# Covariance of the second layer: GpSimd's low parts of six of eight tiles behind the last centred tile, and one load of x issued later

## The chip, the cores and the metric

The kernel is one program on one core of a Trainium2 chip. The metric is the device time of one execution in microseconds. The kernel before takes 867.92 us (median of three runs, 866.33 to 868.16).

## The reference

Two layers, all in float32. The first computes attention weights per pixel and applies them to shifted copies of x; the second is a bottleneck of three convolutions with batch norms and a residual. The change lies in the second, between the second convolution and the end:

```
residual = x
h = relu(bn(conv(x, w1, 1x1), g1, b1))
h = relu(bn(conv(h, w2, 3x3), g2, b2))     # 64 channels
h = bn(conv(h, w3, 1x1), g3, b3)           # 256 channels
return relu(h + residual)                  # (4, 256, 64, 64)
```

`bn` takes mean and variance over batch, height and width of its own input, so the third one needs the statistics of `conv(h, w3)` before the first output can be written.

## The kernel before, in words

The five engines run their own instruction lists, written out by hand, and meet at semaphores (`wait_ge(name, count)`, `then_inc`). There is no scheduler: the order in the code of an engine's block is its order on the chip.

After the second convolution its output lies in `y`, 128 partitions (two groups of 64 channels) by 8 tiles of 1024 pixels. The third batch norm does not run the third convolution first. Its mean and variance are got from the sum of h and from the covariance (Gram) matrix of h, 64 by 64 for each half, through the weights. For that each tile i goes through these steps:

- ScalarE, L1063: batch norm and ReLU of the tile in place, its sum beside it (`relu2`);
- VectorE, L1842: subtracts a constant from the tile (centring), then L1844: casts it to `h2_hi`, the high part of a two-part float32 split. Each counts `centered` up by one, so tile i is done at `centered` 2i + 2;
- GpSimd, L842: the low part, `h2_lo = y - h2_hi`, from two operands in SBUF (`h2_lo_done`);
- TensorE, L1381: transposes each half tile k = 2i, 2i + 1 into PSUM (`hT_ps`), ScalarE L848 (`hT_hi`) and VectorE L1431 (`hT_lo`) split the transposed half, and TensorE L1389 adds it to the Gram matrix (`gram`). On ScalarE the two copies of a tile stand behind the ReLU of the next one.

`hT` has two buffers, so the copies of half tile k wait for the Gram group k - 2.

Then VectorE forms scale and shift of the third batch norm in a chain of small instructions, each waiting for the one before: L1848, L1850 and L1851 on the mean, ahead of the last two `hT_lo`; L1858 to L1865 on the Gram matrix; L1867, L1868, L1869, L1794, a root on ScalarE (L1033), L1797 to L1800. L1850, L1851 and L1794 are tensor_scalars on one or two columns, L1868, L1869 and L1798 to L1800 tensor_tensors with both inputs in SBUF.

The last stage has 32 groups m, four for each of eight output pieces u. TensorE (`last`, L1090 to L1092) multiplies the third weights with `h2_hi` and `h2_lo` of two tiles (0 and 1 for the first two u, 2 and 3 for the next two, and so on); there are four places in PSUM, so group m waits for the addition m - 3. VectorE L1878 scales it and adds x, in the place to which x was loaded (`x1in`, or `y[:, 4:8]` for u = 6). ScalarE L1082 adds the shift, applies the ReLU and writes the result into the place of the piece before (for u = 0 into `y[:, 0:4]`). SyncE stores half a piece after every second group (L509).

The residual x was written by the first layer to memory and comes back in eight loads of 2 MB on SyncE (L712), each issued when its place is free: the seventh (u = 6) goes to `y[:, 4:8]`, so it has to wait for the transposes and the low parts, the eighth for L1867. The stores follow on the same queue.

Of the kernel before, what the change touches and what calls it, by code (L numbers as in the profile page):

```python
# [118 lines left out]
def build(nc, x, w1, b1, w2, b2, v1, g1, c1, v2, g2, c2, v3, g3, c3, out):  # L119
# [6 lines left out]
    with top:  # L126
        def sem(name):
            return top.enter_context(nc.semaphore(name))
# [113 lines left out]
        def x1_place(u):  # L242

            return y[:, 4:8, :] if u == 6 else x1in[:, (2, 3, 4, 5, 6, 1, None, 0)[u], :, :]

        def out_place(u):

            place = x1_place(u - 1) if u else y[:, 0:4, :]
            return place.rearrange("p i e -> p (i e)").rearrange("p (r c) -> p r c", c=W)
# [32 lines left out]
        relu2, h2_lo_done = sem("relu2"), sem("h2_lo_done")  # L282
        c2_done, c2_copied, c2_stat = sem("c2_done"), sem("c2_copied"), sem("c2_stat")
        vT_done, center_done, cov_zero, centered = sem("vT_done"), sem("center_done"), sem("cov_zero"), sem("centered")
        hT_ps, hT_hi_done, hT_lo_done, gram_done = sem("hT_ps"), sem("hT_hi_done"), sem("hT_lo_done"), sem("gram_done")
# [219 lines left out]
        def store_out(sp, u):  # L505
            n, cb = u // 2, u % 2
            for h in range(2):
                sp.wait_ge(f_out, 4 * u + 2 * h + 2)
                sp.dma_start(out[n, cb * P:(cb + 1) * P, 32 * h:32 * h + 32, :],  # L509
                             out_place(u)[:, 32 * h:32 * h + 32, :]).then_inc(out_stored, 16)  # L510
# [17 lines left out]
        def _(sp):  # L528
# [181 lines left out]
            def load_x1(u):  # L710
                n, cb = u // 2, u % 2
                sp.dma_start(x1_place(u), x1_dram[4 * n:4 * n + 4, cb].rearrange("s p e -> p s e")).then_inc(x1_back[u], 16)  # L712
# [5 lines left out]
                load_x1(u)  # L718
            sp.wait_ge(c2_done, 16)
            load_x1(5)  # L720
            sp.wait_ge(hT_ps, 16)
            sp.wait_ge(h2_lo_done, 8)
            load_x1(6)
            sp.wait_ge(sums_ps, 1)
            sp.wait_ge(bn_dve, BN3_READ)
            load_x1(7)
            for u in range(8):
                store_out(sp, u)
            sp.wait_ge(out_stored, 16 * 16)

        @block.gpsimd
        def _(pool):
# [105 lines left out]
            pool.wait_ge(vt_done, 2)  # L838
            pool.memset(cov[:, :], 0.0).then_inc(cov_zero, 1)
            for i in range(8):  # L840
                pool.wait_ge(centered, 2 * i + 2)
                pool.tensor_tensor(h2_lo[:, i, :], y[:, i, :], h2_hi[:, i, :].bitcast(F32), ALU.subtract  # L842
                                   ).then_inc(h2_lo_done, 1)

        @block.scalar
        def _(act):
# [225 lines left out]
            for u in range(8):  # L1072
                cb = u % 2
                if u == 0:
                    act.wait_ge(hT_ps, 16)
                    act.wait_ge(h2_lo_done, 8)
                else:
                    act.wait_ge(f_out, 4 * u)
                for k in range(4):
                    h, a = divmod(k, 2)  # L1080
                    act.wait_ge(f_added, 4 * u + k + 1)
                    act.activation(out_place(u)[:, 32 * h + a:32 * h + 32:2, :].rearrange("p r (c b) -> p b r c", b=2),  # L1082
                                   x1_place(u)[:, 2 * a:2 * a + 2, h * HALF:(h + 1) * HALF].rearrange("p b (r c) -> p b r c", c=SW),
                                   ACT.Relu, bias=shift[:, 2 + cb:3 + cb]).then_inc(f_out, 1)
# [344 lines left out]
        def _(dve):  # L1429
# [328 lines left out]
            def prepare(a):  # L1758
                dve.wait_ge(v_hi_done, 4 * a + 4)
                dve.wait_ge(vT_done, a + 1)  # L1760
                rows = slice(64 * a, 64 * a + 64)
                for k in range(3 * a, 3 * a + 3):
                    (lo, ty), (hi, _) = v2_blocks(v2_lo)[k], v2_blocks(v2_hi)[k]
                    minus(lo, v2_of(rows, ty), hi.bitcast(F32)).then_inc(v_lo_done, 1)
                minus(v3_lo[rows, a, :], psR[1][rows, C:2 * C], v3_hi[rows, a, :].bitcast(F32)).then_inc(v_lo_done, 1)
# [140 lines left out]
```

## Time and profile before

| | |
|---|---|
| median of the runs | 867.92 us |
| profiled execution, its own time | 868.58 us |
| its span | 866.8 us |
| PE busy | 811.2 us (94%) |
| DVE, ACT, POOL busy | 649.2, 376.1, 346.7 us |
| granted clock, mean | 0.98 |
| DMA moved | 162.18 MB, mean 187 GB/s |

The profile is of one execution. PE is TensorE's matmul, PEld its weight load, DVE VectorE, ACT ScalarE, POOL GpSimd, SP SyncE. Times run from the start of the span. The shares are averages over very different stages: the first layer fills about 700 us, the second convolution ends at 774 us, the tiles are centred from 780.6 to 807 us, and the last stage goes from 818.6 us to the end. Only the last 90 us hold anything that the change touches. In these the page's 40 slices show PE at 6, 8, 9, 9 and 6 tenths, and DMA at 9 and more in the last stage but at 0 to 5 while the tiles are centred.

### The profile page before, as it was taken

How to read it: one execution, taken by the hardware profiler on the slowest of the kernel's cores; microseconds unless marked ns; L12 is line 12 of the kernel's file. 1: busy time of each engine (PE TensorE's matmuls, PEld its weight loads, DVE VectorE, ACT ScalarE, POOL GpSimd, SP SyncE). 2: the span in 40 equal slices, each digit the busy share in tenths (PEclk: the TensorE clock that was granted, in tenths of full speed). 3: DMA queues.
4: the chain of work that ended last, by engine and by line, in shares of the span. 5: the costliest groups of instructions: out<-in, count | busy, mean ns of one | idle time of the engine just before them, and what ended most of it. 6: DMA issues, size and time to landing. Idle time of an engine off the chain costs nothing.

```text
span 866.8 us, 13972 instructions
## 1 busy us (share of the span) xinstructions
PE 811.2 (94%) x5084; PEld 770.1 (89%) x5084; DVE 649.2 (75%) x884; ACT 376.1 (43%) x647; POOL 346.7 (40%) x256
## 2 busy tenths in 40 slices
PE   4998988999999999999999999999968989996896
PEld 4997988999999999999999999999968867775685
DVE  4895888898699589868968977896576667129796
ACT  1332112334343434434344444534246697116396
POOL 3318586385267248527723852772200010006200
PEclk9999999999999999999999999999989989998999
DMA  9920515986894996779499688747299995020598
GB/s 265 372 104 0 98 28 132 218 215 171 185 244 123 230 180 193 202 162 243 120 242 174 183 208 168 206 114 211 65 257 264 267 335 236 0 84 14 187 425 358
DMA packets 249932, 162.18 MB, mean 187 GB/s; under 512 B 191833, under 2 KB 232778, under 8 KB 247178
## 3 DMA queue, kind: packets, MB, share of 16 engines
q1 hardware_dynamic: 241162, 144.52, 63.6%
q10 hardware_dynamic: 8704, 16.78, 6.1%
q8 instruction: 42, 0.69, 0.4%
q14 instruction: 24, 0.20, 0.1%
HBM read 99.48 MB, written 56.36 MB: 180 GB/s over the span
## 4 chain that ended last, share of the span: by engine, by line
PE 75%; DVE 8%; issue 5%; POOL 5%; ACT 3%; DMA 3%; SPq 1%; ACTq 0%; DVEq 0%; POOLq 0%
PE ps L1090 21%; PE ps L1092 21%; PE ps L1091 21%; PE ps L1160 4%; PE ps L1176 3%; PE ps L1208 3%; POOL xbuf L778 2%; PE ps L1115 1%; POOL ring L767 1%; DMA w1raw<-in_L_conv_w 1%; DMA raw<-bands 1%; DVE y L1842 1%; POOL whole L762 1%; DVE whole L1519 1%; DVE wsum L1471 1%
## 5 line engine op out<-in xcount | busy, mean ns | idle before, releaser
L767 POOL TENSOR_TENSOR ring<-whole,ring 128x576 fp32r<-128x576 f32 x112 | 188.5, 1687 | 272.9 <-ACT ring L848 272.9
L1090 PE MATMUL ps<-w_hi,ring 128*128 128x336 f32 x832 | 277.7, 334 | 9.4 <-DVE me L1596 7.2
L1092 PE MATMUL ps<-w_hi,ring 128*128 128x336 f32 x832 | 265.3, 319 | 0.0
L1091 PE MATMUL ps<-w_lo,ring 128*128 128x336 f32 x832 | 264.2, 318 | 0.0
L1090 PEld LDWEIGHTS ps<-w_hi,ring 128*128 128x128 f32 x832 | 159.9, 192 | 10.2 <-issue 7.7
L1091 PEld LDWEIGHTS ps<-w_lo,ring 128*128 128x128 f32 x832 | 159.6, 192 | 0.0
L1092 PEld LDWEIGHTS ps<-w_hi,ring 128*128 128x128 f32 x832 | 158.7, 191 | 0.0
L848 ACT ACTIVATE ring<-whole 128x576 fp32r<-128x576 f32 x112 | 87.1, 778 | 107.1 <-POOL whole L762 58.1
L848 ACT ACTIVATE band_hi<-ps 128x320 fp32r<-128x320 f32 (+1 forms) x128 | 53.0, 417 | 127.5 <-PE ps L1160 121.3
L1519 DVE SCALAR_TENSOR_TENSOR whole<-xbuf 128x576 f32<-128x576 f32 x80 | 88.3, 1105 | 14.6 <-POOL ring L767 7.5
L1090 PE MATMUL ps<-band_hi,xT_hi 128*128 128x224 f32 (+2 forms) x320 | 94.9, 297 | 3.2 <-DVE band_lo L1431 3.1
L1091 PE MATMUL ps<-band_lo,xT_hi 128*128 128x224 f32 (+2 forms) x320 | 92.6, 289 | 0.0
L1092 PE MATMUL ps<-band_hi,xT_lo 128*128 128x224 f32 (+2 forms) x320 | 92.6, 289 | 0.0
L778 POOL TENSOR_TENSOR xbuf<-xbuf 128x1152 f32<-128x1152 f32 x32 | 86.5, 2704 | 1.3
L1431 DVE TENSOR_TENSOR band_lo<-ps,band_hi 128x320 fp32r<-128x320 f32 (+1 forms) x128 | 57.4, 455 | 21.5 <-ACT band_hi L848 21.1
L848 ACT ACTIVATE xT_hi<-ps 128x512 fp32r<-128x512 f32 x64 | 37.9, 595 | 79.9 <-PE ps L1176 78.6
L1090 PEld LDWEIGHTS ps<-band_hi,xT_hi 128*128 128x128 f32 x320 | 60.9, 190 | 5.5 <-DVE band_lo L1431 3.7
L1596 DVE SCALAR_TENSOR_TENSOR logit<-ps,logit 128x480 f32<-128x480 f32 x80 | 52.2, 653 | 18.0 <-PE ps L1092 14.4
L1090 PE MATMUL ps<-h_hi,v_hi 128*128 128x512 f32 x160 | 64.8, 405 | 0.6 <-DVE x1in L1878 0.4
L1091 PE MATMUL ps<-h_lo,v_hi 128*128 128x512 f32 x160 | 64.5, 403 | 0.0
L1092 PE MATMUL ps<-h_hi,v_lo 128*128 128x512 f32 x160 | 64.0, 400 | 0.0
L1431 DVE TENSOR_TENSOR xT_lo<-ps,xT_hi 128x512 fp32r<-128x512 f32 x64 | 43.5, 683 | 26.2 <-ACT xT_hi L848 26.2
(165 smaller groups left out, 1370.2 us busy)
## 6 DMA issues: line engine op xcount, KB each, us to landing
xq<-in_x SPq DMA_DIRECT2D x116, 256.0 KB, 4.9
raw<-bands SPq DMA_DIRECT2D x32, 768.0 KB, 7.1
xbuf<-in_x SPq DMA_DIRECT2D x16, 1024.0 KB, 8.7
x_dram<-x ACTq DMA_DIRECT2D x32, 512.0 KB, 4.7
x1in<-x_dram SPq DMA_DIRECT2D x7, 2048.0 KB, 13.3
bands<-wide SPq DMA_DIRECT2D x64, 199.0 KB, 5.4
out<-x1in SPq DMA_DIRECT2D x12, 1024.0 KB, 5.9
w1raw<-in_L_conv_w SPq DMA_DIRECT2D x2, 3136.0 KB, 12.7
```

Of the source, the lines that this page charges most:

```text
L767: pool.tensor_tensor(split(k, 1), positions(whole[:, k % TBUFS, :], 0, 2), split(k, 0).bitcast(F32), ALU.subtract).then_inc(sig_lo_done, 1)
L778: pool.tensor_tensor(a, b, a, ALU.subtract).then_inc(c_done, 1)
L848: return act.activation(dst, src, ACT.Copy)
L1090: pe.matmul(dst, l_hi, r_hi_, start=first, stop=False, **kw)
L1091: pe.matmul(dst, l_hi, r_lo_, start=False, stop=False, **kw)
L1092: return pe.matmul(dst, l_lo, r_hi_, start=False, stop=last, **kw)
L1160: mm = pe.transpose(bank[:, i * P:(i + 1) * P], src, ident[:, :])
L1176: mm = pe.transpose(bank[:, t * C + kb * P:t * C + (kb + 1) * P], src[:, kb, 4 * t:4 * t + 4, g % 2::2], ident[:, :])
L1208: mm = pe.matmul(bank, v1pack[:, cb, :], r[:, cb, :], start=(cb == 0 and j == 0), stop=(cb == CB - 1 and j == 1))
L1431: return dve.tensor_tensor(dst, a, b, ALU.subtract)
L1519: dve.scalar_tensor_tensor(out=dst, in0=a, scalar=factor, in1=b, op0=ALU.mult, op1=ALU.add).then_inc(done, 1)
L1596: dve.scalar_tensor_tensor(out=dst, in0=m, scalar=factor, in1=src, op0=ALU.mult, op1=ALU.add).then_inc(comb_done, 1)
```

## The change

Three edits:

- GpSimd's low parts of tiles 0 and 1 stay where they were. Those of tiles 2 to 7 wait until all eight tiles are centred and cast (`centered` 16) in place of their own tile.
- ScalarE's first instruction of the last stage, which overwrites tiles 0 to 3 of `y`, waits for four low parts in place of eight.
- SyncE's load of x for u = 6, with its two waits, moves from ahead of the load for u = 7 to behind the two stores of the first piece.

```diff
@@ -718,13 +718,14 @@
                 load_x1(u)
             sp.wait_ge(c2_done, 16)
             load_x1(5)
-            sp.wait_ge(hT_ps, 16)
-            sp.wait_ge(h2_lo_done, 8)
-            load_x1(6)
             sp.wait_ge(sums_ps, 1)
             sp.wait_ge(bn_dve, BN3_READ)
             load_x1(7)
             for u in range(8):
+                if u == 1:
+                    sp.wait_ge(hT_ps, 16)
+                    sp.wait_ge(h2_lo_done, 8)
+                    load_x1(6)
                 store_out(sp, u)
             sp.wait_ge(out_stored, 16 * 16)
 
@@ -838,7 +839,7 @@
             pool.wait_ge(vt_done, 2)
             pool.memset(cov[:, :], 0.0).then_inc(cov_zero, 1)
             for i in range(8):
-                pool.wait_ge(centered, 2 * i + 2)
+                pool.wait_ge(centered, 2 * i + 2 if i < 2 else 16)
                 pool.tensor_tensor(h2_lo[:, i, :], y[:, i, :], h2_hi[:, i, :].bitcast(F32), ALU.subtract
                                    ).then_inc(h2_lo_done, 1)
 
@@ -1073,7 +1074,7 @@
                 cb = u % 2
                 if u == 0:
                     act.wait_ge(hT_ps, 16)
-                    act.wait_ge(h2_lo_done, 8)
+                    act.wait_ge(h2_lo_done, 4)
                 else:
                     act.wait_ge(f_out, 4 * u)
                 for k in range(4):
```

SyncE's list at the end of the program (`x_dram` is the copy of x in memory, `y` the place of the load for u = 6; the first two rows are the loads for u = 1 to 4 and u = 5):

```order
 L712 DMA x1in<-x_dram 128x4x1024 x4
 L712 DMA x1in<-x_dram 128x4x1024 [waits c2_done]
-L712 DMA y<-x_dram 128x4x1024 [waits h2_lo_done,hT_ps]
 L712 DMA x1in<-x_dram 128x4x1024 [waits bn_dve,sums_ps]
 L509 DMA out<-y 128x2048 [waits f_out] x2
+L712 DMA y<-x_dram 128x4x1024 [waits h2_lo_done,hT_ps]
 L509 DMA out<-x1in 128x2048 [waits f_out] x12
 L509 DMA out<-y 128x2048 [waits f_out] x2
```

The load into `y` was ahead of the last load into `x1in` and of all stores; now it stands behind the last load and the stores of the first piece, and 14 stores are behind it.

VectorE's list behind the cast of tile 7, as it is in the changed program (all its lines are one further down than before; `gm` and `mv` hold a few columns of statistics, `scale` and `shift` the result):

```order
L1849 TENSOR_REDUCE gm<-sums 128x1
L1851 TENSOR_SCALAR gm<-gm 128x1 [waits bn_dve]
L1852 TENSOR_SCALAR gm<-gm 128x2 [waits bn_dve]
...
L1868 COPY gm<-ps 128x6 [waits sums_ps,bn_dve]
L1869 TENSOR_TENSOR gm<-gm 128x2 [waits bn_dve]
L1870 TENSOR_TENSOR gm<-gm 128x2 [waits bn_dve]
L1795 TENSOR_SCALAR mv<-gm 128x2 [waits bn_dve]
L1798 RECIPROCAL mv<-mv 128x2 [waits bn_act,bn_dve]
L1799 TENSOR_TENSOR scale<-mv,bn 128x2 [waits bn_dve]
L1800 TENSOR_TENSOR mv<-gm,scale 128x2 [waits bn_dve]
L1801 TENSOR_TENSOR shift<-bn,mv 128x2 [waits bn_dve]
L1879 SCALAR_TENSOR_TENSOR x1in<-ps,scale,x1in 128x2x512 [waits f_done,x1_back0,bn_dve]
```

These rows stand in the same order in both programs, and so do GpSimd's eight subtractions; what moved is that six of the eight now start behind the cast of tile 7, and so beside these rows, where there was one.

## Rows read from the trace of the kernel before

**Rows 1.** chain of waits, 776 to 822 us, shares of the stretch by line

```profile
by line: DVE y L1842 18.6%; DVE hT L1431 12.7%; PE ps L1389 9.5%; PE ps L1381 8.2%; issue 7.8%; DVE h_hi L1844 7.8%; ACT y L1063 5.6%; PE ps L1090 4.1%; PE ps L1091 3.6%; PE ps L1092 3.0%; DVE x1in L1878 2.8%; DVE gm L1851 2.1%; ACT hT L848
```

**Rows 2.** VectorE's L1842: durations in ns, least/median/longest

```profile
L1842 DVE TENSOR_SCALAR y<-y,gm x8: 748/1752/1901, 780.6 to 805.3; 128x1024 f32<-128x1024 f32 x8
```

**Rows 3.** timeline of GpSimd, 750 us on: start us, us, what, [idle before]

```profile
793.05 2.39 POOL L842 TENSOR_TENSOR h_lo<-y,h_hi 128x1024 fp32r<-128x1024 f32 x1 [1.36 <-DVE h_hi L1844]
...
808.02 2.38 POOL L842 TENSOR_TENSOR h_lo<-y,h_hi 128x1024 fp32r<-128x1024 f32 x1 [1.36 <-DVE h_hi L1844]
```

**Rows 4.** timeline of VectorE, 773 to 820 us (same columns)

```profile
794.36 1.63 DVE L1842 TENSOR_SCALAR y<-y,gm 128x1024 f32<-128x1024 f32 x1 [0.19 <-ACT y L1063]
796.03 0.69 DVE L1844 CAST h_hi<-y 128x1024 fp32r<-128x1024 f32 x1
...
809.49 0.93 DVE L1851 TENSOR_SCALAR gm<-gm 128x2 f32<-128x2 f32 x1
...
816.95 0.16 DVE L1868 TENSOR_TENSOR gm<-gm 128x2 f32<-128x2 f32 x1
...
818.64 2.48 DVE L1878 SCALAR_TENSOR_TENSOR x1in<-ps,scale,x1in 128x1024 f32<-128x1024 f32 x2
```

**Rows 5.** windows: length, busy PE PEld DVE ACT POOL, clock, DMA share, GB/s

```profile
830.00:834.00 4.00, 4.00 (x19) 3.22 (x18) 4.00 (x4) 4.00 (x4) 0.00 (x0) 1.00 1.02 428
...
865.00:866.00 1.00, 0.00 (x0) 0.00 (x0) 0.00 (x0) 0.00 (x0) 0.00 (x0) 0.50 0.36 148
```

**Rows 6.** timeline of ScalarE, 773 to 820 us

```profile
792.51 0.60 ACT L848 ACTIVATE hT<-ps 128x512 fp32r<-128x512 f32 x1 [0.56 <-PE ps L1389]
793.01 1.24 ACT L1063 ACTIVATE y<-y,shift,scale 128x1024 f32<-128x1024 f32 x1
...
799.20 0.60 ACT L848 ACTIVATE hT<-ps 128x512 fp32r<-128x512 f32 x1 [0.32 <-PE ps L1389]
```

**Rows 7.** timeline of TensorE, 773 to 820 us

```profile
785.58 1.12 PE L1381 MATMUL ps<-ident,y 128*128 128x128 f32 x4 [2.33 <-DVE h_hi L1844]
...
796.78 0.66 PE L1381 MATMUL ps<-ident,y 128*128 128x128 f32 x4 [1.43 <-DVE h_hi L1844]
...
798.38 0.72 PE L1389 MATMUL ps<-hT 128*128 128x256 f32 x4
...
819.98 0.50 PE L1090 MATMUL ps<-h_hi,v_hi 128*128 128x512 f32 x1 [0.41 <-DVE x1in L1878]
```

**Rows 8.** timeline of VectorE, 133 to 138 us

```profile
134.07 1.54 DVE L1633 TENSOR_TENSOR me<-smx,inside 128x112 f32<-128x112 f32 x1
135.65 2.85 DVE L1639 TENSOR_TENSOR wide<-probs,me 128x784 f32<-128x784 f32 x1
```

**Rows 9.** VectorE's L1633: durations in ns, least/median/longest

```profile
L1633 DVE TENSOR_TENSOR me<-smx,inside x8: 274/274/1544, 134.1 to 638.9; 128x112 f32<-128x112 f32 x8
```

**Rows 10.** timeline of GpSimd, 133 to 138 us

```profile
133.36 4.31 POOL L778 TENSOR_TENSOR xbuf<-xbuf 128x1152 f32<-128x1152 f32 x2
```

**Rows 11.** windows, the fall and return of the clock

```profile
785.00:786.00 1.00, 0.42 (x2) 0.43 (x3) 1.00 (x2) 0.15 (x2) 0.40 (x1) 0.50 0.00 0
...
791.00:792.00 1.00, 1.00 (x8) 1.00 (x7) 0.80 (x1) 0.76 (x3) 0.70 (x1) 0.68 0.00 0
```

**Rows 12.** page, part 6: DMA issues, KB each, us to landing

```profile
x1in<-x_dram SPq DMA_DIRECT2D x7, 2048.0 KB, 13.3
...
out<-x1in SPq DMA_DIRECT2D x12, 1024.0 KB, 5.9
```

**Rows 13.** timeline of SyncE's DMA issues, 750 us to the end

```profile
810.47 0.36 SPq L712 DMA_DIRECT2D y<-x_dram  x1
816.99 0.36 SPq L712 DMA_DIRECT2D x1in<-x_dram  x1
822.41 2.74 SPq L509 DMA_DIRECT2D out<-y  x2
...
859.25 3.11 SPq L509 DMA_DIRECT2D out<-y  x2
```

## The prediction

> **What bounds the kernel now.** I read the stretch behind the second convolution (776 us to the end) in this order: the chain of waits, the timelines of VectorE, GpSimd, ScalarE and TensorE, the granted clock, and last the DMA queue of SyncE. In the chain from 776 to 822 us the largest single item is the centring of the tiles, VectorE L1842, with 18.6% [rows 1]. It needs 0.75 us when nothing is in its way, but its median is 1.75 and its longest 1.90 [rows 2]. The reader is to hold two rows side by side: GpSimd's subtraction of 793.05 ends at 795.44 [rows 3], the centring issued at 794.36 ends at 795.99 [rows 4], 0.55 us later. So the centring does not run slowly, it stands until GpSimd's instruction is over and then runs. This is the time the change goes after. Behind it comes the last stage, 32 groups of matmuls, each followed by a VectorE addition, a ReLU and half a store. TensorE is busy in all of it (4.00 of 4.00 us at 830 to 834), VectorE's additions follow it, and the DMA engines are full beside it: share 1.02 and 428 GB/s in the same row [rows 5].
>
> **The sum is made** against the profiled execution: span 866.8, time 868.58, which is 0.66 above the median of 867.92. I write P for the start of GpSimd's last subtraction, 808.02 before [rows 3]; that is just when the last tile is centred and cast.
>
> **What goes: the blocked centrings.** GpSimd still does tiles 0 and 1 at their old places, so up to the centring of tile 2 nothing changes. The centring of tile 3 can start at 791.20 as before. From there a loop over two tiles sets the pace. Centring to cast 0.78 (its 0.75 and a gap), cast to the transposes of that tile 0.75 (796.03 to 796.78), transposes to the second Gram group 1.60 (796.78 to 798.38), Gram to ScalarE's copy 0.82 (to 799.20), copy to ReLU 0.50 (792.51 to 793.01), ReLU to centring 1.35 (793.01 to 794.36) [rows 4, 6, 7]: 5.80 us per two tiles. Tile 4 stays at 794.36, since its ReLU is what it waits for; tile 5 comes at 791.20 + 5.80 = 797.00, tile 6 at 800.16, tile 7 at 802.80 (before: 805.3 [rows 2]). With 0.78 and 0.77 behind it (cast to GpSimd's start), P comes at 804.35: **a gain of 3.65 us.** ScalarE and TensorE, not VectorE, are late next, which is why six freed waits of up to 1.15 us don't all come back.
>
> **What is added: a queue of six on GpSimd.** From P on GpSimd has six subtractions in a row, 2.38 us each [rows 3], 14.3 us in all; before it had one. VectorE's small instructions of the third normalisation lie in that time. One is known: L1851, two elements wide, took 0.93 us and ended at 810.42, GpSimd's instruction at 810.40 [rows 3, 4]. It costs the same in both kernels. The others came when GpSimd was done: L1868, L1869 and L1794 from P + 8.93 on (816.95), and the first addition of the last stage at P + 10.62 (818.64) [rows 4]. Now they meet GpSimd's fourth, fifth and sixth.
> Does a two-input instruction on VectorE stand behind GpSimd too, and who goes first when both queue? The softmax of the first layer shows both. L1633 takes 1.54 us at 134.07, where its least is 0.27, and L1639 right behind it 2.85 [rows 8, 9]; beside them stand two subtractions of GpSimd, 133.36 to 137.67 [rows 10]. Each of the two small ones waited for one of GpSimd's: VectorE gets in between two of them, and then the next of GpSimd's goes ahead of VectorE's next. Applied here: L1868 waits to P + 9.5, L1869 to P + 11.9, L1794 to P + 14.3. From L1794 to the first addition is 1.3 us (L1868, L1869 and L1794 follow each other by 0.20, and the addition follows L1868 by 1.69), so that starts at P + 15.5 and not P + 10.62: **a loss of 4.9 us**. From below: if two elements slip through, nothing is lost; if only one wait is met, 0.6 (L1868 against the fourth) to 2.4 (a whole one). From above: 12 us, if L1851 too must let all six pass. I take 4.9, since the row nearest in kind shows alternation.
> The Trainium skill (SBUF — State Buffer, Who interferes with whom) has the rule for it: the port pair is a lock for a whole instruction, taken by a VectorE instruction in a two-port mode, or with two SBUF inputs against a GpSimd instruction that reads SBUF. The trace agrees for 112 and 784 elements; for two-element tensor_tensors no row before shows it. By that page alone L1798 to L1800 would be at risk as well, but GpSimd is empty by then.
> Together: the last stage starts 4.9 − 3.65 = **1.25 us later**.
>
> **What follows on TensorE.** It computes four groups ahead and then waits for the first addition. That wait was 0.41 us, restart at 819.98 [rows 7]. It becomes about 0.41 + 4.9 = 5.3 us. After the idle stretch of 2.33 us that ended at 785.58 [rows 7] the granted clock was 0.50 at 785 to 786, and it came back inside 791 to 792 (0.68) [rows 11], so about 6 us behind the restart, at the lower of the two levels, 1.2 GHz. Six microseconds at half rate are **3.0 us** of TensorE work, and the last stage follows TensorE. Both ends: 0 (the clock stays), 3.5 (it stays down 7 us). End by TensorE: 866.8 + 1.25 + 3.0 = 871.05.
>
> **What follows for the DMA.** The load of x for tile group 6, 2048 KB [rows 12], went out at 810.47, when the engines were idle [rows 13]. Now it stands in SyncE's order behind both stores of the first output, so at about 826, in the full stretch. It is needed over 20 us later, so nothing waits for it; but all stores behind it do. Bytes from the first store on: 16 stores of 1.049 MB (1024 KB [rows 12]) and 2.10 MB, 18.9 MB, at 428 GB/s [rows 5] 44.1 us. The first store went out at 822.41 [rows 13], now 823.7. In the kernel before the last store is issued at about 862.0 [rows 13] and its bytes end at about 865.4 (148 of some 400 GB/s in 865 to 866 [rows 5]): 3.4 us, of which 2.45 are its 1.049 MB at 428, so 1.0 to the first byte; the span ends 1.4 later. Now the bytes end at 823.7 + 1.0 + 44.1 = 868.8: end by the DMA 870.2. TensorE's 871.05 is the later; with some backlog in front of the last store I take 871.2. Here the two costs cover each other: without the clock's loss the DMA would still hold the end at 870.2. Stores 2.8 us apart (the two issued in 859.25 to 862.36 [rows 13]) ask for 375 GB/s, so a backlog of 2.1 MB shrinks by only 50 GB/s, 1.0 MB in 20 us.
> The Trainium skill (SBUF — State Buffer, Summary: rules for kernel authors) would take 358 GB/s for transfers between HBM and SBUF. By it the 18.9 MB need 52.7 us and the span ends at 878.8. The trace disagrees: it holds 428 [rows 5].
>
> ScalarE's lowered wait (4 in place of 8) is met at P + 4.8, ahead of its first ReLU of the last stage; it only avoids a wait. The low parts of tiles 2 to 7 are wanted by TensorE 5.6 us behind its restart and later, when all are done.
>
> **Forecast:** span 871.2, 4.4 over before; 873.0 for the profiled execution, 872.3 on the scale of the median: slower by 0.5%. Its own range is 870.5 to 874 (clock cost 0 to 3.5, GpSimd's pitch).
>
> **Rivals.**
> 1. *The small instructions are hardly held* (two elements slip through, or one wait in all). For: no row has a two-element instruction with two inputs beside a subtraction of GpSimd. Against: L1851 and [rows 8]. With a loss of 0.6 the stage starts 3.05 earlier and TensorE would end at 863.75, but load 7, the stores and load 6 are then one stream of 21.0 MB, 49.0 us, from 816.99 − 3.65 + 1.0 = 814.3 on: 863.3 + 1.4 and 1.0 for the slower first microseconds of a load, 865.7; with 2.4 it is about 867.9. Time 866.8 to 869.0: mostly no change. 0.20.
> 2. *The DMA has room after all and nothing is held:* 866.8 − 3.65 + 0.6, time 864.9. Against: 428 GB/s is what the full stretch gives. 0.04.
> 3. *GpSimd's queue goes first every time,* place L1851: VectorE is let in at P + 14.3, the Gram matrix of the last tiles comes 12 us late, less 3.65, and 3 for the clock: time 879.2 (11.9 − 3.65 + 3.0 over 867.92). It decides if GpSimd's next instruction is taken ahead of a VectorE one already waiting. Against: [rows 8, 10]. 0.05.
> 4. *The stores are held to 358 GB/s,* as by the rule above: span 878.8, time 879.9. Against: [rows 5]. 0.02.
> 5. *The same mechanism, dearer:* the clock falls twice, or the addition instructions are held too: 874 to 876.5. 0.07.
> The forecast itself has 0.62.
>
> **How the numbers follow.** A change under 0.2% (1.7 us) can't be told from none. Slower: 0.62 + 0.05 + 0.02 + 0.07, 0.76, less 0.04 for the forecast's lower edge: 0.72. Rival 1 gives 0.10 to "same" (with the 0.04: 0.14) and 0.10 to "faster" (with rival 2: 0.14). The range goes from 867.0, inside rival 1, to 875.0, inside rival 5, and leaves out rivals 2 to 4 and part of 1.
>
> **What would show it.** Centrings of tiles 4 to 7 at 0.75 us, and GpSimd's third instruction starting near 804.4: right on the gain. L1868, L1869 and L1794 (each one line further down) with durations of up to 2.4 us: right on the loss. TensorE's idle time ahead of the first group that waits for an addition near 5 us and a clock of 0.50 behind it. 2.1 MB of loads amid the stores, DMA share 1.0 to the end, last store landing later than 4.8 us. The forecast is wrong if the small instructions keep 0.17 us beside a busy GpSimd.

## The result, and the profile after

The changed kernel takes **873.96 us** (median of 5, 873.55 to 876.65) where the kernel before takes 867.92 beside it (866.33 to 869.06): a ratio of **1.0084, 95% interval 1.0067 to 1.0100**, slower. The forecast was 872.3, 4.4 over the kernel before; 6.0 over it were measured, so the sign is right and the size 1.7 us short. The profiled execution took 876.65 (span 874.8), the slowest of the five; 873.0 was forecast for it, with a range of 870.5 to 874, and it lies above that. Of the 8.0 us by which its span exceeds that of the kernel before, 1.5 lie ahead of the first centring, where nothing was changed, and 6.5 behind it. Its lines behind SyncE's edit stand one further down: L1843 is L1842 before.

VectorE's timeline of the changed kernel (start us, us, engine, line, operation, [idle before], with rows left out at the dots):

```profile
792.58 0.75 DVE L1843 TENSOR_SCALAR y<-y,gm 128x1024 f32<-128x1024 f32 x1 [0.53 <-ACT y L1064]
795.17 0.74 DVE L1843 TENSOR_SCALAR y<-y,gm 128x1024 f32<-128x1024 f32 x1
...
807.21 0.93 DVE L1852 TENSOR_SCALAR gm<-gm 128x2 f32<-128x2 f32 x1
...
814.67 0.46 DVE L1869 TENSOR_TENSOR gm<-gm 128x2 f32<-128x2 f32 x1
815.16 2.32 DVE L1870 TENSOR_TENSOR gm<-gm 128x2 f32<-128x2 f32 x1
817.51 2.27 DVE L1795 TENSOR_SCALAR mv<-gm 128x2 f32<-128x2 f32 x1
...
820.91 6.05 DVE L1879 SCALAR_TENSOR_TENSOR x1in<-ps,scale,x1in 128x1024 f32<-128x1024 f32 x5
```

The centrings of tiles 3 to 7 run in 0.75 us and no longer stand behind GpSimd, as the one in [rows 4] did: the first row above (tile 3) waits for ScalarE's ReLU, the second (tile 4) only for VectorE's own work ahead of it. In exchange three instructions two elements wide (L1869, L1870, L1795) take 0.46, 2.32 and 2.27 us; the first of them took 0.16 before [rows 4]. GpSimd's timeline shows what they stand behind:

```profile
787.08 2.38 POOL L843 TENSOR_TENSOR h_lo<-y,h_hi 128x1024 fp32r<-128x1024 f32 x1 [0.63 <-DVE h_hi L1845]
805.74 14.02 POOL L843 TENSOR_TENSOR h_lo<-y,h_hi 128x1024 fp32r<-128x1024 f32 x6 [16.28 <-DVE h_hi L1845]
```

Six subtractions in 14.02 us are 2.34 each, so the fourth, fifth and sixth end near 815.1, 817.4 and 819.8; the three small instructions end at 815.13, 817.48 and 819.78.

TensorE's timeline, and windows of it (length, busy PE, PEld, DVE, ACT, POOL, clock, DMA share, GB/s):

```profile
822.25 0.79 PE L1091 MATMUL ps<-h_hi,v_hi 128*128 128x512 f32 x1 [4.97 <-DVE x1in L1879]
```

```profile
820.00:822.00 2.00, 0.00 (x0) 0.00 (x0) 1.74 (x5) 0.02 (x1) 0.00 (x0) 0.77 0.72 291
822.00:824.00 2.00, 1.75 (x4) 1.46 (x5) 2.00 (x3) 1.69 (x2) 0.00 (x0) 0.50 0.04 16
824.00:826.00 2.00, 2.00 (x6) 1.52 (x6) 2.00 (x3) 2.00 (x3) 0.00 (x0) 0.50 0.27 115
826.00:828.00 2.00, 2.00 (x7) 1.53 (x6) 1.19 (x2) 1.97 (x2) 0.00 (x0) 0.52 1.00 406
828.00:830.00 2.00, 2.00 (x10) 1.64 (x9) 1.75 (x2) 1.23 (x2) 0.00 (x0) 1.00 1.05 381
830.00:834.00 4.00, 4.00 (x18) 3.19 (x18) 3.65 (x4) 3.25 (x4) 0.00 (x0) 1.00 0.95 312
834.00:838.00 4.00, 4.00 (x19) 3.21 (x18) 3.58 (x4) 3.65 (x4) 0.00 (x0) 1.00 1.00 310
838.00:842.00 4.00, 4.00 (x19) 3.23 (x18) 3.72 (x4) 3.51 (x4) 0.00 (x0) 1.00 1.01 426
...
872.00:873.00 1.00, 0.00 (x0) 0.00 (x0) 0.00 (x0) 0.00 (x0) 0.00 (x0) 0.50 0.22 90
873.00:874.00 1.00, 0.00 (x0) 0.00 (x0) 0.00 (x0) 0.00 (x0) 0.00 (x0) 0.50 0.08 33
```

TensorE idles 4.97 us, its clock is 0.50 (1.2 GHz) from about 821 to 828, and comes back 5.7 us behind the restart at 822.25. The last two columns, on the DMA engines, are the part to look at twice. Before, they moved 428 GB/s in 830 to 834 [rows 5]. Here, in 830 to 838, they are as busy (share 0.95, 1.00) and move 312 and 310. SyncE's timeline has the moved load there, and the page's part on DMA issues (KB each, us from issue to landing) has stores that land in 10.2 us, not 5.9 [rows 12]:

```profile
824.74 2.69 SPq L509 DMA_DIRECT2D out<-y  x2
827.53 0.40 SPq L712 DMA_DIRECT2D y<-x_dram  x1
830.35 31.27 SPq L509 DMA_DIRECT2D out<-x1in  x12
```

```profile
out<-x1in SPq DMA_DIRECT2D x12, 1024.0 KB, 10.2
y<-x_dram SPq DMA_DIRECT2D x1, 2048.0 KB, 12.6
```

**One measure for all runs.** The first centring starts between 778.2 and 784.1 us in the profiles of this study, a scatter that lies ahead of the place of the change. So I cut each profiled execution at three marks: C, the first centring's start; P, GpSimd's subtraction right behind the last cast; A, the first addition of the last stage. All differences are of rows in the timelines. Each row is one profiled execution; the three kernels that were profiled twice agree within 0.1, 0.3 and 0.5 us from C to the end, so less than half a microsecond in the last column is not read.

| kernel | C to P | P to A | A to end | C to end | against before |
|---|---|---|---|---|---|
| before | 27.40 | 10.62 | 48.16 | 86.18 | |
| after | 23.64 | 15.17 | 53.89 | 92.70 | +6.5 |
| after, again (e10) | 23.74 | 15.19 | 53.88 | 92.81 | +6.6 |
| load late alone (e1; e11) | 27.42; 27.42 | 10.62; 10.63 | 54.71; 54.41 | 92.75; 92.46 | +6.6; +6.3 |
| load not late (e2) | 23.63 | 15.21 | 50.73 | 89.57 | +3.4 |
| three subtractions held (e3) | 23.74 | 10.62 | 54.22 | 88.58 | +2.4 |
| one held, load not late (e7) | 23.59 | 13.07 | 52.54 | 89.20 | +3.0 |
| e2 with a busy TensorE (e6) | 22.92 | 15.26 | 49.25 | 87.43 | +1.3 |
| extra stores (e5; e12) | 27.43; 27.40 | 10.63; 10.61 | 52.09; 51.67 | 90.15; 89.68 | +4.0; +3.5 |
| load on another queue (e8) | 27.41 | 10.62 | 52.26 | 90.29 | +4.1 |
| four pieces, order 4 to 7 first (e4) | 23.64 | 10.91 | 48.52 | 83.07 | −3.1 |
| three early, four pieces (e9) | 24.06 | 10.94 | 48.66 | 83.66 | −2.5 |

### The profile page after: what moved, and what is told of

It reads as the page before. It is cut to its first block, busy times and chain, and to the rows that moved or that the text cites. A ratio compares the mean times of both kernels' runs of the same rounds, so it can differ in the third digit from the quotient of the medians.

```text
span 874.8 us, 13972 instructions
## 1 busy us (share of the span) xinstructions
PE 814.6 (93%) x5084; PEld 773.2 (88%) x5084; DVE 650.3 (74%) x884; ACT 376.1 (43%) x647; POOL 345.9 (40%) x256
## 4 chain that ended last, share of the span: by engine, by line
PE 78%; DVE 8%; issue 4%; POOL 4%; ACT 2%; DMA 2%; SPq 0%; ACTq 0%; DVEq 0%; POOLq 0%
PE ps L1091 21%; PE ps L1093 21%; PE ps L1092 21%; PE ps L1161 4%; PE ps L1177 3%; PE ps L1209 3%; POOL xbuf L779 2%; PE ps L1116 1%; POOL ring L768 1%; DMA w1raw<-in_L_conv_w 1%; POOL whole L763 1%; DVE whole L1520 1%; PE ps L1340 1%; DVE wsum L1472 1%; PE ps L1390 1%
## 5 line engine op out<-in xcount | busy, mean ns | idle before, releaser
L1091 PEld LDWEIGHTS ps<-band_hi,xT_hi 128*128 128x128 f32 x320 | 61.1, 191 | 5.3 <-DVE band_lo L1432 3.7
## 6 DMA issues: line engine op xcount, KB each, us to landing
out<-x1in SPq DMA_DIRECT2D x12, 1024.0 KB, 10.2
```

Source lines behind the costliest of these rows:

```text
L1091: pe.matmul(dst, l_hi, r_hi_, start=first, stop=False, **kw)
```

## The experiments

The theory: GpSimd's queue and VectorE's small instructions take turns (P to A), and the clock's fall costs TensorE 3 us. The first rival: the end is set by the DMA engines, and the late load costs more than its bytes. The second: the small instructions have another cause. Each diff shows the lines that matter, against the kernel before unless said; dots stand for lines left out.

**e1_load_only** moves the load alone; GpSimd keeps its places.

```diff
-            sp.wait_ge(hT_ps, 16)
-            sp.wait_ge(h2_lo_done, 8)
-            load_x1(6)
...
             for u in range(8):
+                if u == 1:
+                    sp.wait_ge(hT_ps, 16)
+                    sp.wait_ge(h2_lo_done, 8)
+                    load_x1(6)
                 store_out(sp, u)
```

> The kernel before with the load of x for u = 6 alone moved behind the first two stores; GpSimd's subtractions stay at their places. Theory A (the DMA engines hold the end once 2.1 MB more stand in the full stretch): first store still near 822.4 counted as in the kernel before, DMA share 1.0 to the end, 21.0 MB from about 818 on at 428 GB/s end near 868, so the span grows by 2 to 3 us (ratio 1.002 to 1.004), and by 4 to 5 if the rate dips to some 310 GB/s for 8 us as in the profile of the changed kernel. TensorE's idle stretch ahead of the fifth group stays near 0.4 us and the clock at 1.00. Theory B (the load is hidden, the whole loss comes from GpSimd's queue): ratio within 0.999 to 1.001.

Measured: 872.71, ratio 1.0064 (1.0040 to 1.0089). TensorE is not delayed at all, the last store is issued 54.0 us behind P as before, and the end still comes 6.5 us later. Its windows from 826 us and at the end:

```profile
826.00:828.00 2.00, 2.00 (x10) 1.62 (x9) 2.00 (x2) 2.00 (x3) 0.00 (x0) 1.00 0.99 311
828.00:830.00 2.00, 2.00 (x10) 1.60 (x9) 2.00 (x3) 1.97 (x3) 0.00 (x0) 1.00 0.95 360
830.00:834.00 4.00, 4.00 (x19) 3.23 (x18) 3.95 (x4) 3.97 (x4) 0.00 (x0) 1.00 0.99 299
834.00:838.00 4.00, 4.00 (x19) 3.23 (x18) 3.58 (x4) 3.66 (x4) 0.00 (x0) 1.00 1.03 432
...
868.00:869.00 1.00, 0.00 (x0) 0.00 (x0) 0.00 (x0) 0.00 (x0) 0.00 (x0) 0.50 0.68 287
869.00:870.00 1.00, 0.00 (x0) 0.00 (x0) 0.00 (x0) 0.00 (x0) 0.00 (x0) 0.50 0.23 98
870.00:871.00 1.00, 0.00 (x0) 0.00 (x0) 0.00 (x0) 0.00 (x0) 0.00 (x0) 0.50 0.06 25
```

The dip is there without GpSimd's edit, and the last bytes trickle for 3 us. In the profile the load alone costs as much as the whole change; by times it costs 5.3 us, more than the 4 to 5 expected with a dip.

**e2_load_ahead** is the changed kernel with this load ahead of the first store:

```diff
             load_x1(7)
+            sp.wait_ge(hT_ps, 16)
+            sp.wait_ge(h2_lo_done, 8)
+            load_x1(6)
             for u in range(8):
                 store_out(sp, u)
```

> The changed kernel with the load for u = 6 put between the load for u = 7 and the first store, so that it goes out when the last low part is done, some 14 us behind the last cast, and fills the stretch in which the DMA engines were idle. Theory A (queue on GpSimd 4.6, clock 2.4, less 3.7 gained, set TensorE's end at +3.3; the load adds what is above that): the DMA is no longer behind TensorE, span about 3.3 to 3.8 us over the kernel before (ratio 1.004 to 1.0045), last store landing in 4 to 5 us, not 10. Theory B (the place of the load among the stores does not matter, its bytes cost the same anywhere in the last stage): the same as the changed kernel, 1.007 to 1.0085.

Measured: 870.92, 1.0042 (1.0022 to 1.0063). Its TensorE idles 5.00 us and the clock is 0.50 as in the changed kernel, but no dip is seen (422 GB/s in 830 to 834) and stores land in 5.6 us. What is left, +3.4 us of the profile, is TensorE's side alone: counted from C, the last store is issued 3.4 us later than before, and the end follows it by 4.8 us in both.

**e3_hold** adds to the changed kernel a wait on GpSimd: tiles 5 to 7 come behind the third normalisation.

```diff
+                if i == 5:
+                    pool.wait_ge(bn_dve, BN3_END)
```

> The changed kernel with GpSimd's last three subtractions (tiles 5 to 7) held until the scale and shift of the third normalisation are done; those of tiles 2 to 4 run right behind the last cast. Theory A (small VectorE instructions stand behind GpSimd's): L1869, L1870 and L1795 of the changed kernel take about 0.17 us each, the first addition comes 10.6 us behind the last cast and not 15.2, TensorE's idle time stays near 0.4 us and its clock at 1.00; TensorE's end is 3.7 us ahead of the kernel before. The late load then holds the end by the DMA: 0.5 to 1 us ahead of the kernel before if the rate is 428 GB/s, up to 2 us behind it if it dips (ratio 0.999 to 1.002). Theory B (the loss came from the transfers alone, the small instructions were slow for another reason): the first addition again about 15 us behind the last cast, ratio 1.006 or more.

Measured: 870.11, 1.0037 (1.0016 to 1.0057). VectorE's timeline:

```profile
811.49 0.16 DVE L1871 TENSOR_TENSOR gm<-gm 128x2 f32<-128x2 f32 x1
811.69 0.16 DVE L1872 TENSOR_TENSOR gm<-gm 128x2 f32<-128x2 f32 x1
811.88 0.17 DVE L1797 TENSOR_SCALAR mv<-gm 128x2 f32<-128x2 f32 x1
```

With GpSimd idle, the same three take 0.16 to 0.17, P to A is 10.62 again, TensorE idles 0.41. The second rival falls. Yet the kernel is slower than before, though its last stage starts 3.66 us sooner, and it misses the upper end that was expected (1.002): the load is late here too (252 GB/s at 828 to 830) and A to end is 54.22, near e1's.

**e5_more_stores** leaves the load at its old place and adds two stores of 1 MB, a second copy of the first output piece to a tensor of its own, behind the first two stores.

```diff
+                if u == 1:
+                    for h in range(2):
+                        sp.dma_start(extra[h], out_place(0)[:, 32 * h:32 * h + 32, :]).then_inc(extra_stored, 16)
                 store_out(sp, u)
```

> The kernel before with 2.1 MB of stores added behind the first two (the first piece stored once more, to a tensor of its own), where the run with the moved load had a 2.1 MB read. Load and GpSimd as before. That run ended 6.5 us later than before counted from the last low part, of which the bytes alone explain some 2.8; its rate fell to 230 to 365 GB/s for 8 us. Theory A (a read amid the stores costs more than its bytes): with writes in its place the rate stays at 410 to 440 GB/s through the whole stretch, and since the read is now spared as well (it was done in idle time), the span grows by 2.5 to 3.5 us (ratio 1.003 to 1.004). Theory B (any deeper queue makes the engines drop, read or write): a dip as before and 5 to 6.5 us (ratio 1.006 to 1.0075).

Measured: 871.13, 1.0038 (1.0019 to 1.0057). The same bytes as the load, from the other direction, and no dip:

```profile
828.00:830.00 2.00, 2.00 (x10) 1.61 (x9) 2.00 (x3) 1.97 (x3) 0.00 (x0) 1.00 1.01 426
830.00:834.00 4.00, 4.00 (x19) 3.23 (x18) 3.95 (x4) 3.97 (x4) 0.00 (x0) 1.00 1.02 430
834.00:838.00 4.00, 4.00 (x19) 3.22 (x18) 3.58 (x4) 3.64 (x4) 0.00 (x0) 1.00 1.02 428
```

So about 4 us of the load's 6.5 come from 2.1 MB more in a stretch that has no room, whichever way they go (2.5 to 3.5 were expected of the run). The rest goes with what sets the load apart from these stores: first of all that it is a read, but it is also one transfer of 2 MB in place of two of 1 MB, at other addresses.

**e6_busy** is e2 with the matmuls of group 3 done four times over (the result is the same), so that TensorE has work while it would wait.

```diff
-                for b in range(2):
+                for b in (0, 1) * (4 if m == 3 else 1):
```

> The run with the load ahead of the stores, and TensorE kept busy in its idle stretch: the matmuls of the fourth group are run four times over (the same values into the same place, the signal behind the last), 4.2 us more of work in 5.0 us of waiting. Theory A (the idle stretch lowers the clock to 0.50 for 5 to 6 us, worth 2.4 us of TensorE work, on the path to the end): idle time under 1 us, clock 1.00 from 815 to 862, last store issued some 2.4 us earlier counted from the last cast, span 2.0 to 2.4 us shorter than without (ratio to before 1.0015 to 1.0025 where that one had 1.0042). Theory B (the clock costs nothing, since the DMA sets the end anyway): ratio 1.004 again.

Measured: 870.01, 1.0029 (1.0010 to 1.0047). TensorE idles 0.85, the clock stays 1.00, P to A is 15.26 as in e2, and the last store is issued at P + 58.7, not P + 61.2. So in the profiles the clock's fall costs 2.5 us of TensorE. Not all of it reaches the end: P to the end is 64.51 here and 65.94 in e2, 1.4 less, and the end comes 5.9 us behind the last store where it comes 4.8 behind in e2 and before, as the DMA engines have a backlog again. By times the two can't be told apart (1.0029 and 1.0042, with intervals that overlap), and 1.0029 lies over the 1.0015 to 1.0025 expected.

Its C to P is 0.7 shorter than e2's, and the clock says where that comes from. In this execution it stays at 1.00 from 784 to 794, though TensorE idles 2.33 us there as in every other profile; in the other thirteen it falls to 0.50. The first transposes behind that idle time take 0.66 us, not e2's 1.12, and the centring of tile 3 comes at C + 9.76, not C + 10.48.

**e7_hold_one** is e2 with only tile 7 held.

```diff
+                if i == 7:
+                    pool.wait_ge(bn_dve, BN3_END)
```

> The run with the load ahead of the stores, but GpSimd's last subtraction alone (tile 7) held until scale and shift are done. Five run behind the last cast. Theory A (VectorE is let in between two of GpSimd's, one at a time): the first of the three small instructions ends at about P + 9.4, the second at P + 11.7, the third takes 0.17 us as nothing is left on GpSimd, and the first addition comes at about P + 13.0, 2.3 us behind the kernel before and not 4.6. TensorE waits some 2.8 us, about as long as the one in the centring stage behind which the clock did fall; the load goes out later, at P + 15.5. Ratio 1.000 to 1.003. Theory B (GpSimd's queue must be empty before VectorE is let in): all three short, the wait in one piece.

Measured: 870.70, 1.0039 (1.0023 to 1.0055).

```profile
812.30 0.48 DVE L1870 TENSOR_TENSOR gm<-gm 128x2 f32<-128x2 f32 x1
812.82 2.31 DVE L1871 TENSOR_TENSOR gm<-gm 128x2 f32<-128x2 f32 x1
815.16 0.17 DVE L1796 TENSOR_SCALAR mv<-gm 128x2 f32<-128x2 f32 x1
```

One subtraction fewer in GpSimd's queue is one wait of 2.3 us fewer on VectorE, and A comes at P + 13.07. This is the alternation, instruction by instruction. TensorE still idles 2.90, up to 817.80, and its clock falls here too: 0.67 at 818 to 820 and 0.50 at 820 to 822. That and the load keep the ratio above the 1.000 to 1.003 expected. The load is issued 1.2 us ahead of the first store here; the stores caught up with it (231 GB/s at 824 to 826), and A to end is 52.54 where e2 has 50.73.

**e8_other_queue**: the load of e1, issued from ScalarE's queue behind the first output's work; its old place on SyncE is taken out.

```diff
+                if u == 1:
+                    act.dma_start(x1_place(6), x1_dram[12:16, 0].rearrange("s p e -> p s e")).then_inc(x1_back[6], 16)
```

> The kernel before with the load for u = 6 at the same late point, behind the first two stores, but issued by ScalarE on its own queue instead of SyncE's. Theory A (the loss comes from reads and writes sharing the 16 engines and the memory, whatever queue they are in): the dip and the late end stay, ratio 1.005 to 1.0075 like the load on SyncE's queue (1.0064). Theory B (the order within one queue is what costs, the stores behind the load waiting for it): the dip is gone, the loss is that of the bytes, ratio 1.002 to 1.0035.

Measured: 871.73, 1.0056 (1.0037 to 1.0075). The dip is shallower (340 at 828 to 830, 406 at 830 to 834) and the load lands in 18.4 us; in the profile it costs 4.1 us, 2.5 less than e1 and 2.2 less than e11. By times it can't be told from e1.

**e11_load_again** and **e12_stores_again** repeat e1 and e5, which ran on two chips, side by side on a third, since the difference between them carries the verdict on reads.

> The kernel before with the load alone moved behind the first two stores, again, to be set against the run with 2.1 MB more of stores on the same chip. Theory A (a read amid stores costs more than its bytes): 0.8 to 1.5 us slower than that run, ratio 1.0055 to 1.0065, a dip in the rate while it runs. Theory B (only bytes count): the two within 0.4 us.

> The kernel before with 2.1 MB more of stores behind the first two, again. Bytes at 428 GB/s give 2.5 to 2.8 us; the first run of it had 4.1. If a full queue at the end costs by itself (the last store lands in 10 us and the last megabyte runs out slowly), the 4 us come again, ratio 1.004 to 1.005, rate 410 to 440 GB/s until 3 us before the end and a thin rest behind. If 4.1 was scatter, ratio 1.003.

Measured: 873.30, 1.0065 (1.0045 to 1.0085), with dips to 297 and 324; and 871.48, 1.0050 (1.0029 to 1.0072), with none (430 in 830 to 834). In the profiles the read costs 2.6 us more than the stores the first time and 2.8 the second; the medians differ by 1.6 and 1.8 (0.8 to 1.5 were expected), and the intervals of the ratios overlap. So the profiles show the difference, twice; the times alone don't.

**e10_changed_again** repeats the changed kernel; nothing is edited.

> The changed kernel once more, beside the two that take its transfer apart and more runs of the kernel before. Theory A (the last stage starts 0.9 us later by 4.6 lost and 3.7 gained, and the load amid the stores then adds some 5): ratio 1.0065 to 1.0075; in its profile P at 3.7 us ahead of the kernel before counted from the first centring, the first addition 15.2 us behind P, and a stretch of 4 to 8 us at 230 to 360 GB/s while the load runs. Theory B (the first profile, with its long end, was an exceptional run, and the typical one has neither dip nor long end): ratio near 1.005, which would be the forecast's own number.

Measured: 876.56, 1.0093 (1.0069 to 1.0118), over the 1.0065 to 1.0075 expected. Its times lie in two groups (872.78 and 873.21; 876.4 to 877.65), as did the first five. The two profiles are one of each, 872.78 and 876.65: behind C they agree within 0.1 us, and C itself is 3.9 us apart. In these two the groups arise ahead of the change. One thing differs behind C: TensorE idles 4.99 us and restarts at 818.45, and the clock is back at about 822.7, 4.3 us later and not 5.7. The last store is issued at P + 60.5 in place of P + 61.1, and the end is the same, which fits an end set by the DMA engines.

**e4_pieces** and **e9_three_early** are the version that the runs point to: the freed centrings kept, VectorE's small chain left alone, and the load early. The load overwrites the centred tiles 4 to 7, so GpSimd takes these first, and the load goes in four pieces, each as its tile is done. What is left is held behind the normalisation. e9:

```diff
+            for j in range(4):
+                sp.wait_ge(h2_lo_done, 4 + j)
+                sp.dma_start(y[:, 4 + j, :], x1_dram[12 + j, 0]).then_inc(x1_back[6], 16)
...
-            for i in range(8):
-                pool.wait_ge(centered, 2 * i + 2)
+            for i in (0, 1, 2, 4, 5, 6, 7, 3):
+                pool.wait_ge(centered, 2 * i + 2 if i < 3 else 16)
+                if i == 3:
+                    pool.wait_ge(bn_dve, BN3_END)
```

In lines not shown TensorE, ScalarE and VectorE wait for the counts that go with it. e4 has the order 0, 1, 4, 5, 6, 7, 2, 3 and holds two.

> GpSimd's order is tiles 0, 1 at their places, then 4, 5, 6, 7 right behind the last cast, then 2 and 3 behind scale and shift; the load for u = 6 is cut into four pieces of 0.5 MB, each issued when the low part of its tile is done and ahead of the load for u = 7. Theory A: the small chain loses at most 0.6 us (it meets the end of the fourth subtraction), no clock loss, the 2.1 MB flow before the stores, and the whole gain of the centring stage is kept: span 3.0 to 3.7 us under the kernel before, ratio 0.996. Theory B (some other bound, as the DMA, holds the last stage whatever is done): ratio 0.999 to 1.001.

> The faster order with one tile more at its old place: GpSimd does tiles 0, 1, 2 as in the kernel before, 4 to 7 right behind the last cast, 3 behind scale and shift; load in four pieces. ScalarE then need not wait for the low part of tile 3 before the second half of the first piece (its store came 1.1 us late with two tiles held back). The centring of tile 3 stands again behind GpSimd, 0.3 us, and tile 4 is held by its ReLU anyway. Theory A: the same time or up to 0.5 us less than with two tiles held back, ratio 0.996 to 0.9975. Theory B (the blocked centring runs on through the loop of two tiles): 0.3 us more, 0.9975 to 0.998.

Measured: 865.52, 0.9972 (0.9956 to 0.9988), and **864.73, 0.9964 (0.9946 to 0.9982)**, 12 times each. GpSimd's timeline of e9, and its DMA issues:

```profile
788.65 2.39 POOL L845 TENSOR_TENSOR h_lo<-y,h_hi 128x1024 fp32r<-128x1024 f32 x1 [1.36 <-DVE h_hi L1849]
804.00 9.40 POOL L845 TENSOR_TENSOR h_lo<-y,h_hi 128x1024 fp32r<-128x1024 f32 x4 [12.96 <-DVE h_hi L1849]
815.05 2.39 POOL L845 TENSOR_TENSOR h_lo<-y,h_hi 128x1024 fp32r<-128x1024 f32 x1 [1.65 <-DVE shift L1805]
```

```profile
806.46 7.29 SPq L724 DMA_DIRECT2D y<-x_dram  x4
813.85 0.38 SPq L712 DMA_DIRECT2D x1in<-x_dram  x1
818.72 2.71 SPq L509 DMA_DIRECT2D out<-y  x2
```

The load is out before the first store, P to A is 10.94, TensorE idles 0.75, and A to end is 48.66, 0.5 over before. Both beat the kernel before, e4 by a little less than the 0.996 expected; between them the intervals don't decide. Several things change at once here, so these two show that the version works and not what each part of it brings.

## Why the prediction was right in sign and short in size

1. **What goes, a gain of 3.65 us.** Measured 3.76 and 3.66 (C to P 23.64 and 23.74 for 27.40). The pace is the loop over two tiles that was forecast: centrings at 792.58 and 798.38 are 5.80 apart. Right, but for tiles 4 and 6: tile 4 was to stay where it was, for its ReLU, and comes 0.7 us sooner (C + 13.07, before C + 13.74), as that ReLU is earlier too. Tile 7 comes at C + 22.08 for 22.18 forecast, so nothing hangs on it.
2. **What is added, a loss of 4.9 us.** Measured 4.55 (P to A 15.17 for 10.62); the waits are 0.46, 2.32 and 2.27, for the fourth, fifth and sixth subtraction in turn. e3 takes the cause away and the loss goes; e7 takes one instruction away and one wait goes. Right. The rule that I named from the Trainium skill (SBUF — State Buffer, Who interferes with whom) is borne out by these rows for two elements as well. Rivals 1 and 3 did not come about, nor did 2 and 4 (the engines moved 426 GB/s on average from 838 to 872); rival 5 had room for the size, but neither of its reasons is seen.
3. **TensorE, 3.0 us by the clock.** The idle time was forecast at 5.3 and is 4.97; the cost is 2.5 of TensorE's time (e6 against e2), of which 1.4 reach the end. e2 shows the sum of this side: 0.8 later at A and 2.6 behind it, +3.4, where the forecast had 1.25 + 3.0. Right in kind, 0.8 high. How long the clock stays down was one number in the forecast, 6 us; behind the same idle time of 5 us it was 5.7 and 4.3 in the two profiles of the changed kernel.
4. **The step that failed is "What follows for the DMA": the end by the DMA was put at 870.2, below TensorE's 871.05, and so it didn't count.** Counted from C as in the kernel before, TensorE's side ends at 870.2 (e2) and the changed kernel at 873.3: the later end is the DMA's, and it was put 3 us too early. I priced the load by its bytes at 428 GB/s, and took the end as 1.4 us behind the last full-rate byte. By that arithmetic (first store + 1.0 + 44.1 + 1.4) the changed kernel would end at 871.2 from its own first store at 824.74; it ended at 874.8, 3.6 later. Two things fill this. The four windows from 826 to 838 are 1.07 MB short of 428 GB/s (0.04 + 0.09 + 0.46 + 0.47), which is 2.5 us. The remaining 1.1 us fits the run-out: 90 and then 33 GB/s from 872 to 874, where before one window of 148 was the last [rows 5]. e1 has both without any work on TensorE being later, and e5 has no dip and costs 2.6 us less than e1.
5. **The two costs cover each other,** the forecast said, and that held, only with the other one on top, the DMA's: A to end is 53.89 with the clock's fall and 54.71 and 54.41 without it. The sum that holds is −3.76 + 4.55 + 5.73 = +6.5 us, of which the load alone explains all (e1 +6.6), and TensorE's side alone 3.4. The medians say 6.0.

What I could have seen: no row before has a load amid stores in the full stretch, so its price was unknown, and I bounded GpSimd's waits from both sides but not this one. The forecast's own list of what would show it had "last store landing later than 4.8 us"; the row to fear was the one in the middle.

**Open.** Which property of the load among stores lowers the rate: its direction is suggested by e5 and e12, and another queue makes the dip shallower (e8), but piece sizes and addresses were not varied apart. Why the queue runs out slowly after a long full stretch. Why the part ahead of C scatters by up to 5.9 us; it may also be what keeps the ratio between 1.0067 and 1.0100. Why the clock fell behind an idle time of 2.33 us in thirteen profiles and not in e6's.

## What to carry to other kernels

When an edit moves a transfer, ask first whether the stretch it lands in has room; where the DMA share is 1.0, a load of 2.1 MB cost 6.3 to 6.6 us here, and its bytes at 428 GB/s are 4.9. A load that is wanted late may be better issued early, in pieces as its buffer comes free, as in e4 and e9. Work moved off one chain of a shared engine lands beside another: list the small instructions of the other engine that fall into the new queue, and price each at up to one whole instruction of it. Compare profiles from a mark just ahead of the change, not from the start of the program.

## What the runs showed of the hardware that I had not expected

- A load amid stores took the DMA from 428 down to some 300 GB/s for eight microseconds or a little less, with the engines busy throughout (share 0.95 to 1.01; 312 and 310 in the changed kernel, 311, 360 and 299 in e1, 297, 401 and 324 in e11).
- The same 2.1 MB as stores leave the rate at 430 and still cost 3.5 to 4.0 us behind the first addition (e5, e12).
- TensorE's clock fell to 1.2 GHz with an idle time of 2.90 us (e7) as with 4.97, and came back some 4 us behind the restart there (817.80 to about 822), 5.7 in the changed kernel and 4.3 in its repetition. With an idle time of 2.33 us in the centring stage it fell in thirteen of fourteen profiles, and not in e6's.
- An instruction of VectorE of 128 x 1 elements beside a busy GpSimd was not held: L1851 took 0.21 us at 806.96 in the changed kernel, just ahead of L1852 with its 0.93.
